# One check-free load of each block limit, a product wait on ScalarE, and one pacing wait per block on GpSimd

## The reference

```python
h = jnp.maximum(_layernorm(x, axis=-1), 0.0)
Qv = h @ W_Q.T ; Ku = h @ W_K.T
score = einsum('md,md->m', Qv[dst], Ku[src]) / sqrt(D) * exp(-edge_weight)
# per target node: keep the 16 best edges, softmax over them
agg = segment_sum(alpha[:, None] * (h[src] @ W_msg.T), dst, n)
x = x + relu(h @ W_self.T + agg)
```

## Time and profile before

| | |
|---|---|
| median of 3 runs | 2024.26 us (2023.76 to 2025.97) |
| span of the profiled execution | 2021.2 us |
| PE / DVE / ACT / POOL busy | 1406.6 / 1485.8 / 1073.1 / 1492.9 us |
| gathers (POOL, L610) | 1564 |
| queue q0 (gathers) | 102.80 MB |

### The profile page before, as it was taken

How to read it: one execution, slowest core, us unless ns; L and a number is a source line. 1 busy time by engine, 2 the same in 40 slices (tenths; PEclk the granted TensorE clock), 3 DMA queues, 4 the chain that set the end, 5 groups by cost and what they waited for, 6 DMA issues and landing times.

```text
span 2021.2 us, 48472 instructions
## 1 busy us (share of the span) xinstructions
PE 1406.6 (70%) x15219; PEld 1293.2 (64%) x15220; DVE 1485.8 (74%) x5024; ACT 1073.1 (53%) x3376; POOL 1492.9 (74%) x1577
## 2 busy tenths in 40 slices
PE   1157888767767677767767766776777677777776
PEld 0147778667666666666666766666766666666765
DVE  6668999676777767676776867777676767777766
ACT  3767666545555455554545545554554545455553
POOL 7776777777777777777777777777777777777773
PEclk9968999888888887888888889888888987887887
DMA  8832334333333333333333233333333333333321
GB/s 231 281 92 84 115 106 115 98 90 101 86 101 90 97 102 87 102 87 99 90 97 101 87 101 86 101 91 97 102 88 100 89 99 88 99 102 87 100 74 33
DMA packets 120627, 206.05 MB, mean 102 GB/s; under 512 B 32268, under 2 KB 75922, under 8 KB 120172
## 3 DMA queue, kind: packets, MB, share of 16 engines
q0 software_dynamic: 50112, 102.80, 19.8%
q1 hardware_dynamic: 69627, 97.27, 14.8%
q10 hardware_dynamic: 626, 2.84, 0.4%
HBM read 186.34 MB, written 16.44 MB: 100 GB/s over the span
## 4 chain that ended last, share of the span: by engine, by line
DVE 36%; issue 20%; DMA 15%; PE 14%; POOL 6%; ACT 4%; POOLq 2%; SPq 1%; ACTq 0%; DVEq 0%
DVE s L896 10%; DMA X<-H_table,idx 6%; DMA E<-H_table,idx 5%; PE pS L1285 5%; DMA Z<-H_table,idx 4%; DVE Dm L920 4%; DVE X L891 4%; DVE D L789 4%; POOL X L610 3%; PE pU L1278 2%; PE pT L1242 2%; POOL Z L610 2%; POOL E L610 2%; PE pS L1242 2%; ACT X L1149 2%
## 5 line engine op out<-in xcount | busy, mean ns | idle before, releaser
L610 POOL DMA_INDIRECT X<-H_table,idx x662 | 627.6, 948 | 205.8 <-issue 157.6
L1149 ACT ACTIVATE X<-OT,w 128x125 f32<-128x125 bf16 x1792 | 530.0, 386 | 30.7 <-DVE w L970 30.7
L610 POOL DMA_INDIRECT E<-H_table,idx x437 | 414.5, 949 | 141.7 <-issue 110.3
L1121 ACT ACTIVATE OT<-pT 128x512 bf16<-128x512 f32 (+1 forms) x500 | 274.6, 549 | 399.5 <-PE pT L1253 388.3
L610 POOL DMA_INDIRECT Z<-H_table,idx x403 | 382.7, 950 | 123.8 <-issue 92.4
L1253 PE MATMUL pT<-identb,O 125*128 125x128 bf16 x1800 | 212.1, 244 | 306.7 <-DVE X L891 255.5
L1253 PEld LDWEIGHTS pT<-identb,O 125*128 125x128 bf16 x1800 | 133.5, 108 | 358.3 <-issue 274.9
L1242 PE MATMUL pG<-G,O 125*128 125x128 bf16 x3600 | 313.8, 250 | 0.0
L1242 PEld LDWEIGHTS pG<-G,O 125*128 125x128 bf16 x3600 | 275.8, 115 | 0.1
L896 DVE TENSOR_REDUCE s<-X 128x8 f32<-128x1024 f32 x200 | 268.3, 1342 | 0.0
L1285 PE MATMUL pS<-Dm,OT 128*128 128x145 bf16 x1800 | 196.2, 287 | 0.4 <-DVE Dm L920 0.4
(11 more groups left out here) (197 smaller groups left out, 2488.5 us busy)
## 6 DMA issues: line engine op xcount, KB each, us to landing
rawi<-D_table SPq DMA_DIRECT2D x50, 576.0 KB
ewt<-D_table SPq DMA_DIRECT2D x50, 576.0 KB
X<-H_table,idx POOLq DMA_INDIRECT x662
E<-H_table,idx POOLq DMA_INDIRECT x437
Z<-H_table,idx POOLq DMA_INDIRECT x403
hb<-H_table SPq DMA_DIRECT2D x100, 62.5 KB
xb<-in_x SPq DMA_DIRECT2D x100, 62.5 KB
out<-ob SPq DMA_DIRECT2D x100, 62.5 KB
```

Source lines behind the costliest of these rows:

```text
L610: return eng.indirect_dma_start(out=Et[q][:, t * 128:(t + 1) * 128], out_offset=None, in_=x if b < RAW else H, in_offset=bass.IndirectOffs ...
L1121: AT.mark(eng.activation(OT[b % 3][:, q0[g]:q0[g] + GQ[g], :].rearrange("p t n -> p (t n)"), pT[:, 0:GQ[g] * 128], ACT.Copy), b, f"T{g}")
L1149: last = eng.activation(weighted(c)[:, t * 128:t * 128 + NB], OT[c % 3][:, t, 0:NB], ACT.Copy, scale=w[:, t:t + 1])
```

## The change

Three things are done.

- SyncE and GpSimd read the limits with `values_load` without the runtime check of the value, and each only once: SyncE keeps the register from `meta(b)` for `spread(b)`, GpSimd keeps the upper limit of block b as the lower one of block b + 1. ScalarE's load in `share` loses its check as well.
- ScalarE's `share(b)`, for b > 2, waits for the moment `s4` of block b - 1 on DVE instead of for eight landings and `s_er`.
- GpSimd's `in_step` keeps the wait at u = 6 alone.

```diff
+        def first_edge(engine, b):
+            return nc.values_load(alrow[0:1, b:b + 1], engines=[engine], min_val=0, max_val=M,
+                                  skip_runtime_bounds_check_because="a count of the M targets, rounded down")
...
+            begins = {}
+
             def meta(b):
                 q = b % NM
                 PA.wait(eng, b - NM, "mT")
-                r = eng.value_load(alrow[0:1, b:b + 1], min_val=0, max_val=M)
+                begins[b] = r = first_edge(mybir.EngineType.SP, b)
...
             def spread(b):
                 q = b % 2
                 VO.wait(eng, b - 2, "O2")
-                r = eng.value_load(alrow[0:1, b:b + 1], min_val=0, max_val=M)
-                eng.dma_start(dB[q][:, :], D16[0:1, bass.ds(r, CAP)].to_broadcast([128, CAP])).then_inc(s_db[q], 16)
+                eng.dma_start(dB[q][:, :], D16[0:1, bass.ds(begins.pop(b), CAP)].to_broadcast([128, CAP])).then_inc(s_db[q], 16)
...
+            bounds = {}
+
             def edges_of(b):
-                r0 = eng.value_load(alrow[0:1, b:b + 1], min_val=0, max_val=M)
-                r1 = eng.value_load(alrow[0:1, b + 1:b + 2], min_val=0, max_val=M)
+                r0 = bounds.pop(b) if b else first_edge(mybir.EngineType.Pool, 0)
+                bounds[b + 1] = r1 = first_edge(mybir.EngineType.Pool, b + 1)
                 return eng.snap(r1 - r0, min_val=0, max_val=M)
 
             def in_step(b, t):
                 lead = max(0, LEAD_AT - b * LEAD_LESS // 10)
                 a, u = divmod(b * SURE + t - lead, SURE)
-                if u == 1:
-                    PX.wait(eng, a - 1, "Gx4")
-                elif 1 < u < 6:
-                    PM.wait(eng, a - 3, f"agg{u - 2}")
-                elif u == 6:
+                if u == 6:
                     AU.wait(eng, a - 3, "U")
-                elif u == 7:
-                    PT.wait(eng, a, "T0")
-                elif u == 8:
-                    PG.wait(eng, a, "Gx0")
-                elif u == 9:
-                    PG.wait(eng, a, "Gx1")
-                elif u == 10:
-                    PT.wait(eng, a, "T2")
-                elif u == 11:
-                    PG.wait(eng, a, "Gx2")
-                elif u == 12:
-                    PW.wait(eng, a - 2, "Wx")
-                elif u == 13:
-                    VM.wait(eng, a - 1, "D")
-                elif u == 14:
-                    PG.wait(eng, a, "Gx3")
-                elif u == 15:
-                    VF.wait(eng, a - 3, "fin")
...
             def share(b):
 
-                for t in range(SURE - AHEAD, SURE):
-                    landed(eng, b - 1, t)
-                eng.wait_ge(s_er, b)
+                if b > 2:
+                    VM.wait(eng, b - 1, "s4")
+                else:
+                    for t in range(SURE - AHEAD, SURE):
+                        landed(eng, b - 1, t)
+                    eng.wait_ge(s_er, b)
                 PM.wait(eng, b - NE, "agg3")
-                at = eng.value_load(cprow[0:1, b:b + 1], min_val=0, max_val=(T - 1) * 128)
+                at = nc.values_load(cprow[0:1, b:b + 1], engines=[mybir.EngineType.Activation], min_val=0, max_val=(T - 1) * 128,
+                                    skip_runtime_bounds_check_because="a difference of two row numbers, clamped to (T - 1) * 128")
```

## The result

The changed kernel takes 2015.23 us (median, 2014.03 to 2016.74) against 2025.12 (2023.76 to 2026.19) for the kernel before, run beside it: a ratio of 0.9949, 95% interval 0.9937 to 0.9961, some 10 us faster. The forecast was 2017.8 us, 6.5 us faster. On the chip of the first eight experiments the kernel before takes 2564 us, and there the changed one is 26% *slower*. Each experiment says which kind of chip it ran on. I call them the quick chips (before: 2024 to 2026 us; those of the result and of two more sets of runs) and the other chip (before: 2564 us). The changed kernel as it stands ran on a quick chip only for the result above; on the two later quick chips only versions of it ran.

What follows compares the result with a forecast made beforehand. GpSimd's unbroken run of gathers, 1.25 us each, was taken as the bound. Start 5.9, ScalarE 0.4 and late steps 0.2 us sum to 6.5 us off 2024.26: 2017.8 us, range 2013.5 to 2023 for 8 in 10.

Steps and rivals of the forecast that it cites:

- The bound, and the steady step: GpSimd's gathers from block 7 on: an unbroken run at 1.25 us each, a step the change leaves as it is.
- rival C: GpSimd's steady run: the step is the sequencer's after all, so 105 us go, about 1915 us; chance 0.03.
- The start: GpSimd, block 7: gathers begin 7.45 us earlier, then u = 6 holds tile 14 until 176.30; gain 5.9 us.
- ScalarE: `share` on the way to `U` of blocks 1 and 2: 0 to 0.8 us less, taken as 0.4 us.
- The new wait for `s4`: ScalarE's `share`: the wait is already met when ScalarE gets there, cost 0.
- The late steps and the long issues: GpSimd's steady run: fewer instructions take away 0 to 3.5 us of late steps, counted as 0.2 us.
- In the steady run they are worth nothing: GpSimd's some 14 removed waits per block: 0.24 us of sequencer time a block, hidden behind the gathers, gain 0.
- Rival D: Whole kernel: late steps and ScalarE's full 0.8 us add to the start, 10.2 us, 2014 us; forecast with it 0.73.
- SyncE: SyncE's queue is off the path; the destinations' broadcast is issued about 1 us earlier, and that hides.
- rival B: GpSimd, tile 5: the moved broadcast delays tile 1's landing in every block, 27 us more, 2045 us; chance 0.06.
- Rival A: Opening: earlier gathers slow DVE, so `U` of blocks 1 and 2 comes later; head start lost, 2022 us; chance 0.18.
- keep their 1.25 us step, since no wait bounds it today: GpSimd: all 1440 gathers behind the earlier start keep their step, so the 5.9 us gain reaches the end.

Runs made afterwards that it cites:

- the first eight experiments: Eight kernels run on the other chip: single parts of the change, doubled waits, the changed kernel again, and it without pacing waits; ratios there from 0.9958 to 1.2596.
- e11: Changed kernel, each gather from block 9 on fetching 256 bytes per row instead of 512: 2013.91 us, ratio to before 0.9942, quick chip.
- e2: Kernel before with ScalarE's `share` part of the change alone: 2553.25 us, ratio to before 0.9958, other chip.
- e10: Changed kernel, pacing waits u = 10 and u = 14 put back from block 8 on: 2015.12 us, ratio to before 0.9947, quick chip.
- e12: Changed kernel with all 15 pacing waits from block 8 on, only u = 6 before: 2019.38 us, ratio to before 0.9964, quick chip.
- e3: Kernel before with the changed loads of SyncE and GpSimd alone: 2564.32 us, ratio to before 0.9991, other chip.
- e9: Changed kernel, from block 9 on GpSimd waits for the previous gather's landing ahead of tiles 4, 8, 12, 15: 2858.35 us, ratio to before 1.4100, quick chip.
- e6: Kernel before with each pacing wait issued twice: 2573.59 us, ratio to before 1.0050, other chip.

## Why the prediction was right, and where not

**The bound, and the steady step.** Right on the quick chip. The step stayed at 1.25 us with 14 waits, one load and two checks fewer, so the sequencer is not the bound (rival C), and `e11` shows that the DMA's bytes aren't either.

**The start.** Right in mechanism and nearly in size: the wait u = 6 took over, at tile 14 of block 7. I had 176.30 for it, it came at 175.45, 6.74 us earlier than before in place of 5.89. It is the sum of two errors against each other. The gather followed `U` of block 1 (174.68) by 0.77 us, not by 0.35, since the release I had taken as a measure was that of another wait. And that `U` was 1.27 us earlier, not 0.4. In block 8 no wait was left (`U` of block 2 ends at 188.96, the gather starts at 190.45, 12 steps behind the other): 6.79 us earlier, where I had 5.94. Block 7 began at 155.97, not 157.25, because `idx` was earlier by 1.28 us too; the 0.87 us behind it was exact. That the size came out so near is luck in part: `e11`, with the same opening, has tile 14 at 177.63, only 4.56 us earlier than the kernel before.

**ScalarE.** The term of the sum that was mis-sized. I priced the two shares on the way at 0.15 us each, the check alone, and took 0.4 us in all. They gave 0.84 - 0.58 = 0.26 and 0.94 - 0.42 = 0.52 us, 0.78 us together; and since these two still wait for the landings, I put it down to the check and what hangs on it; no run takes the check out alone. The remaining 0.49 us of the 1.27 lies in the opening, 0.61 us earlier ahead of both shares (0.12 are lost again behind them), and the opening differs from run to run (`idx` of block 5 was written between 111.25 and 113.91 us in the five kernels that are alike up to there). The later shares gave more than I had allowed: the 28 that copy X to X wait 5.7 us in place of 21.2, 0.55 us each, where I had at most 0.43. On the quick chips it doesn't reach the time (1808.6 and 1809.6 us above); on the other one `e2`, where the check and the new wait change together, is 0.4% faster. The new wait for `s4` cost nothing that shows.

**The late steps and the long issues.** Priced at 0.2 between 0 and 3.5 us. The late steps gave 1.6 and the gathers' durations, of which I had no term, 1.2; `e10` to `e12` put the waits' share at 2 to 3 us. "In the steady run they are worth nothing" was wrong by that much. What makes a step late the traces don't show, but they do show where: at the same tiles in every kernel. The two longest stand at tile 5 of blocks 46 and 85, at 938.06 and 1705.06 in the kernel before (1.23 and 1.51 us of idle time) and at 930.32 and 1695.55 in the changed one (shown above). `e10`, `e11` and `e12` have late steps at the same two gathers, and smaller ones stand, not in every trace, at tile 6 of blocks 33, 59, 72 and 98; these six blocks are 13 apart. The Trainium skill (Runtime: NRT & Kernel Launch, Instruction fetch mechanics) says that an engine's instructions are refilled in blocks of 256, mostly hidden. By that rule, with the records of GpSimd's sequencer between 500 and 1900 us down from 1967 to 617, late steps that come from refills would be fewer and at other tiles. The trace agrees with fewer (3.45 to 1.84 us) and not with other tiles, so it doesn't bear the rule out as their cause. Rival D, the change brings more than the start, is what happened (2014 forecast for it, 2015.2 measured), its number partly by luck: it had 3.5 us from the late steps, which gave 1.6, and nothing from the durations.

**SyncE.** Right. The broadcast is issued 0.47 us behind `hb` in place of 1.29, and no step at tile 5 is late that wasn't (rival B).

**Rival A** didn't come: DVE worked 172.55 of 180 us beside the earlier gathers, and a gather took 134.71 / 143 = 0.94 us. From 156 to 164 us, where the gathers are new, DVE's longest reduction (128x1280) took 1.48 us as before. The Trainium skill (SBUF — State Buffer, SBUF: two separate sides) has a VectorE instruction in a two-port mode and GpSimd's writing of descriptors keep each other out. By that rule the gathers beside a fuller DVE would have lengthened; this trace doesn't show it, nor whether any of these instructions ran in such a mode.

**What no part of the prediction covered** is the other chip. The one sentence that decides it is "keep their 1.25 us step, since no wait bounds it today". It was read from one trace of one chip, and on the other chip the same waits carry the schedule. The sign of the result depends on where the kernel runs: -0.5% on the quick chip, where two versions of it on a second quick chip gave the same (`e10`, `e11`), +26% on the other. Of the versions run, `e2_share_only` is faster than the kernel before on the other chip (0.9958); it wasn't run on a quick one. `e12_start_and_rest` keeps 7 of the 10 us on a quick chip; on the other one only its parts were measured, and their product, 1.0126 x 0.9958 x 0.9991 = 1.0075, is an estimate.

## What to carry to other kernels

Where one engine issues at a fixed step from an early moment to the end, read when the unbroken run starts and which wait will be the last one once the first is gone; here that gave the start to within a microsecond, and the edits behind the fixed step gave 3 us of 1808. A pacing wait that is always met in the trace isn't thereby useless: time its removal on more than one chip. And a latency is to be taken from a wait of the same kind: `U` to gather was 0.77 us where `T2` to gather is 0.35, and landing to gather made a step of 3.53 us in the mean where I had 2.6.

## What was not expected of the hardware

- The same program takes 2024 to 2026 us in three sets of runs on quick chips and 2564 in two sets on the other, with GpSimd's step inside a run of gathers at 1.25 us on both. The mean granted clock of TensorE is 0.86 on the quick chip, 0.77 on the other (`e3`) and 0.68 there for the changed kernel. In the block shown above it is still at 1.00 when TensorE comes to a stop at 1440 us, and falls to its lower level (0.50, that is 1.2 GHz) from 1444 us on, so it need not be the cause. On the quick chip the long pauses of `e9` bring the same 0.77.
- There TensorE's results reach ScalarE and DVE late while GpSimd issues gathers without a break: 16.19 us (median) behind the recorded end for `pAW` in the changed kernel, 1.41 us with all the waits (`e3`), 0.01 us on the quick chip.
- A gather of 128 rows keeps GpSimd busy for 0.947 us with 256 bytes per row (`e11`) and for 0.947 us with 512 (the changed kernel), from 500 to 1900 us.
- Waits that are met cost little: 15 more per block (`e6`) made 0.5% on the other chip, and the 14 per block of the kernel before 2 to 3 us of 1808 on the quick ones.
- On the quick chips the longest late steps of GpSimd stand at the same gathers in all kernels, whatever its sequencer has between them (tile 5 of blocks 46 and 85 in five traces, of 0.8 to 1.9 us).
